# Adding half of the experts' results on GpSimd inside the attention, in a tuned one-core transformer kernel

## The chip, the cores and the metric

One core of a Trainium2 chip. The metric is the device time of one execution, from its first to its last instruction, in microseconds (us). TensorE is called PE below, VectorE DVE, ScalarE ACT, GpSimd POOL and the DMA queue's engine SP, as in the profile.

## The reference

The input x holds 8 batches of 512 rows of 128 channels. Two blocks follow each other, cut here to their steps:

```python
x = x + 0.5 * L0_ffn(layernorm(x))            # 8 experts, top 2, capacity 256
x = x + L0_attn(layernorm(x))                 # 16 heads, keys and values from a strided convolution
x = x + 0.5 * L0_ffn(layernorm(x))
x = x + 0.5 * L1_ffn(x)                       # its own causal attention, then 16 experts, top 2
x = x + L1_attn(x)                            # 16 heads, causal
x = x + 0.5 * L1_ffn(x)
```

A layer with experts gives every row the outputs of two experts, each times a gate: `out = out + combine[:, e][:, None] * ye`. The second block works on twice as many shorter sequences in the reference's own setup, but all calls here get (8, 512, 128).

## The kernel before

All of x stays in SBUF, as 32 tiles of 128 rows (four a batch). The program runs blocks one after the other; each ends with a barrier for all engines: experts, attention 1 (with convolution), experts, attention 2 (causal, the one inside the first L1_ffn, whose rows are normalised twice: once for the residual, once for the projections), experts, attention 3 (two attentions in a row, causal, 16 batches counted together), experts, and an end block that adds the last results and stores them.

**Experts.** `moe` ends with SP loading each row's two expert outputs back from DRAM, into the tiles xn and hid (`k.back`), 512 rows a batch. `k.rv[:, 4]` and `k.rv[:, 5]` hold the gates. Their addition into x is left to the block that follows.

**Attention.** `attention` is written as one program per engine. The unit of work is (batch b, group g of four heads), u = 4b + g, with 4 units a batch. For each unit PE computes the scores twice: first as row maxima (`max_tile`, L373 with the masks of L358), which DVE reduces (L657), and later as score products (`score_chunk`, L482) transposed, whose exponentials ACT writes (L530), and which PE multiplies with the values (L427). The maxima of a unit go PE transpose (L382), ACT copy (L562), a split into three bf16 parts on POOL (`max_split`, L767 to L773), and by SP into three rows of the query operand in SBUF (`put_max`, L872); the unit's first score product waits for them. A query and a key are themselves split into three bf16 parts (`split` on POOL, `split_first_keys` on DVE for batch 0), written to DRAM (`write_parts`, L854) and loaded back, laid out by group, by `load(b, g)` (L864), which also gates the maxima of that unit.

`order(u)` lists what happens in unit u: score chunk i, then the maxima tile i of unit u + 2 in another bank of PSUM, then the events whose number in the table `when` is i. PE, ACT and DVE all walk through the same list and each does its share. Chunks number 8 in attention 1 and 12 in the causal ones. Three PSUM banks take the maxima in turn, so that PE's tile i needs DVE's tile i - 3. POOL and SP have hand-written loops: POOL's unit u is `max_split(u + 1)`, then copies of value rows (`spread`), then one of: normalising batch b + 2 (g = 0), adding the output bias to its residual rows (`add_bias`, g = 1), splitting its queries and keys (g = 3). SP starts with

```python
            load(0, 0)
            load(0, 1)
            put_max(0)
            load(0, 2)
            load(0, 3)
            write_parts(1, 0)
```

**The entry.** Before the units DVE brings the batches in, in the groups 0, 1, 2 to 3 and 4 to 7 (`ENTRY_GROUPS`). `enter` adds the two gated results of each batch (`combine`, L251, four tiles each), takes means and variances (`moments`, L145 and L148) and ends with a chain of small operations for 1/sqrt (`deviations`, L156 and L115 to L119; twice over in attention 2, L160 to L164). `norm(b)` writes the normalised rows to transpose (xa) and, in attention 2, the residual rows (hid). Batches from 2 on are normalised on POOL. DVE's order is: enter 0, norm 0, enter 1, (convolve 0), norm 1, split_first_keys, value rows of batch 0, (convolve 1), enter the group 2 to 3, the maxima of unit 0, enter the group 4 to 7, the maxima of unit 1, then the units. The rows of batch 4 are first needed by POOL in unit 8.

## Time and profile before

| | |
|---|---|
| median of 3 runs | 2228.93 us (2227.15 to 2235.24) |
| the profiled execution | 2219.2 us |
| its span | 2217.5 us |
| PE busy | 1635.7 us (74%) |
| DVE busy | 1380.3 us (62%) |
| POOL busy | 1014.6 us (46%) |
| ACT busy | 979.6 us (44%) |

The span runs from the first to the last instruction of the profiled execution; the time beside it is what the device reports for the same execution. Attention 1 begins at about 150 us, attention 2 at 613 and attention 3 at 1254. A line of a timeline merges neighbouring instructions of one kind: its start, its length, engine, line, operation, what it writes and reads, the number of instructions, and in brackets the idle time of the engine before it with what ended it. In a list of waits stand the total, the number of times and the longest.

### The profile page before, as it was taken

To read this page: it belongs to the slowest core of one execution; us is meant where nothing else is said; L and a number is where in the kernel's file an instruction comes from. 1 tells how busy PE (TensorE), PEld (TensorE's weight loads), DVE (VectorE), ACT (ScalarE), POOL (GpSimd) and SP (SyncE) were. 2 spreads that over 40 slices of the span, in tenths; PEclk is the share of its full clock that TensorE was granted. 3 is DMA by queue.
4 is the path that set the end of the run, shared out by engine and by line. 5 is a ranking of instruction groups with operands and counts; after the bars stand their busy time and mean duration, and the time that the engine had idled before them with its cause. 6 is when DMAs were issued, how large, how long until landed. Compare 5 with 4: busy or idle time off the path is not lost. (4 is left out here: it accounts for less than half of the span.)

```text
span 2217.5 us, 45287 instructions
## 1 busy us (share of the span) xinstructions
PE 1635.7 (74%) x16814; PEld 929.4 (42%) x16816; DVE 1380.3 (62%) x3344; ACT 979.6 (44%) x2064; POOL 1014.6 (46%) x1706
## 2 busy tenths in 40 slices
PE   4434778873637999982687359999999999836872
PEld 3321333332514656651333135555656556523331
DVE  8538667746188777757321497777777777474213
ACT  1112566651214766661222127667666767511220
POOL 1233365530523657430577334536556674305772
PEclk9975899985858999996898669999999999867996
DMA  6242222210432323300244322332323233002444
GB/s 199 65 126 74 57 70 72 76 38 27 139 86 60 103 79 84 103 22 24 62 102 87 104 84 75 92 85 75 103 71 92 79 89 98 22 24 58 95 86 129
DMA packets 226872, 178.20 MB, mean 80 GB/s; under 512 B 33447, under 2 KB 215599, under 8 KB 226272
## 3 DMA queue, kind: packets, MB, share of 16 engines
q1 hardware_dynamic: 211232, 154.74, 24.6%
q0 software_dynamic: 10240, 17.96, 4.0%
q8 instruction: 135, 2.21, 0.4%
q10 hardware_dynamic: 5184, 2.63, 0.4%
q14 instruction: 81, 0.66, 0.1%
HBM read 104.34 MB, written 72.35 MB: 80 GB/s over the span
## 5 line engine op out<-in xcount | busy, mean ns | idle before, releaser
L657 DVE TENSOR_REDUCE mx<-PS 128x2 f32<-128x512 f32 (+3 forms) x1408 | 787.6, 611 | 255.5 <-PE PS L358 171.3
L530 ACT ACTIVATE pt<-PS 128x512 f32<-128x512 f32 (+2 forms) x1408 | 667.1, 533 | 363.7 <-PE PS L358 263.4
L373 PE MATMUL PS<-ka,qa 48*128 48x256 bf16 (+3 forms) x2048 | 503.6, 308 | 86.7 <-DVE mx L657 80.1
L482 PE MATMUL PS<-qa,ka 51*128 51x512 bf16 (+3 forms) x1792 | 485.2, 319 | 31.3 <-DMA qa<-nm 31.2
L358 PE MATMUL PS<-mask_q,identh 64*128 64x128 bf16 (+1 forms) x3072 | 354.9, 206 | 0.0
L427 PE MATMUL PS<-pt,vs 128*32 128x512 f32 (+3 forms) x3584 | 348.6, 482 | 0.0
L358 PE MATMUL PS<-mask_k,identh 64*128 64x64 bf16 (+1 forms) x3072 | 343.3, 202 | 0.0
L1174 POOL DMA_INDIRECT pt<-xn_rows,idx x160 | 165.3, 1033 | 333.7 <-DVE idx L1109 286.1
L767 POOL CAST nm<-nm 16x128 bf16<-16x128 f32 x128 | 36.0, 281 | 593.3 <-ACT nm L562 581.2
L358 PEld LDWEIGHTS PS<-mask_k,identh 64*128 64x128 bf16 x3072 | 270.3, 95 | 54.1 <-issue 1.8
L358 PEld LDWEIGHTS PS<-mask_q,identh 64*128 64x128 bf16 x3072 | 275.3, 97 | 26.5 <-issue 6.8
L482 PEld LDWEIGHTS PS<-qa,ka 51*128 51x128 bf16 x1792 | 166.7, 94 | 262.9 <-issue 153.6
L1025 ACT ACTIVATE pt<-PS,f1b 128x512 f32<-128x512 f32 x128 | 88.0, 687 | 314.3 <-PE PS L981 314.3
L373 PEld LDWEIGHTS PS<-ka,qa 48*128 48x128 bf16 x2048 | 173.8, 95 | 107.1 <-DVE mx L657 90.8
L991 PE MATMUL PS<-pt 128*128 128x512 f32 (+1 forms) x384 | 158.4, 558 | 0.0
L981 PE MATMUL PS<-pt 128*128 128x512 f32 (+1 forms) x384 | 153.0, 544 | 3.1 <-DVE pt L1137 2.0
L427 PEld LDWEIGHTS PS<-pt,vs 128*32 128x32 f32 x3584 | 81.4, 109 | 90.2 <-issue 39.4
L981 PEld LDWEIGHTS PS<-pt 128*128 128x128 f32 x384 | 76.4, 200 | 71.4 <-issue 62.7
L1145 DVE COPY qa<-PS 128x512 f32<-128x512 f32 (+1 forms) x48 | 28.9, 603 | 115.6 <-PE PS L991 115.6
L991 PEld LDWEIGHTS PS<-pt 128*128 128x128 f32 x384 | 74.3, 204 | 56.7 <-issue 54.1
L1183 POOL DMA_INDIRECT y_rows<-pt,idx x80 | 79.7, 996 | 38.4 <-issue 22.0
L391 PE MATMUL PS<-ident,xa 128*128 128x128 f32 x128 | 24.1, 320 | 97.0 <-DVE xa L188 80.2
(212 smaller groups left out, 2363.0 us busy)
## 6 DMA issues: line engine op xcount, KB each, us to landing
pt<-in_f_w SPq DMA_DIRECT2D x96, 256.0 KB, 3.2
q_parts<-parts SPq DMA_DIRECT2D x192, 128.0 KB, 2.4
qa<-q_parts SPq DMA_DIRECT2D x256, 96.0 KB, 2.4
k_parts<-parts SPq DMA_DIRECT2D x144, 128.0 KB, 2.4
ka<-k_parts SPq DMA_DIRECT2D x192, 96.0 KB, 2.4
xn_rows<-xn SPq DMA_DIRECT2D x32, 256.0 KB, 2.3
xn<-y_rows SPq DMA_DIRECT2D x32, 256.0 KB, 4.8
hid<-y_rows SPq DMA_DIRECT2D x32, 256.0 KB, 5.4
```

The lines of the kernel that those rows point to most:

```text
L358: mm = pe.matmul(PS[:, bank, col + lo:col + hi], k.identh[half * HALF:(half + 1) * HALF, j, :], table[half * HALF:(half + 1) * HALF, j, lo ...
L373: mm = pe.matmul(PS[:, bank, i * n:(i + 1) * n], k.qa[rows, b % 2, g, h // 2, qb * P:(qb + 1) * P], k.ka[rows, b % 2, g, h // 2, 0:n], sta ...
L427: mm = pe.matmul(PS[32 * h:32 * h + 32, O_BANK, q0:S], k.vs[:, g, kb, h, :], k.pt[:, u % 2, at[c] + i * n:at[c] + (i + 1) * n], start=(kb ...
L482: mm = pe.matmul(PS[:, bank, i * n:(i + 1) * n], k.ka[rows, b % 2, g, h // 2, kb * P:(kb + 1) * P], k.qa[rows, b % 2, g, h // 2, q0:S], st ...
L530: nc.scalar.activation(k.pt[:, u % 2, at[c]:at[c] + len(heads) * n], PS[:, SC_BANK + c % RING, 0:len(heads) * n], ACT.Exp, scale=SCORE_SCA ...
L657: nc.vector.tensor_reduce(out, PS[:, MX_BANK + t % RING, 0:len(heads) * n] .rearrange("p (h n) -> p h n", n=n), AX.X, ALU.max).then_inc(s. ...
L767: pool.tensor_copy(hi, full).then_inc(s.nm_hi.h, 1)
L981: pe.matmul(PS[:, H_BANK + f, 0:capacity], k.w1[:, par, f * P:(f + 1) * P], k.xeT[:, par, 0:capacity], start=True, stop=True).then_inc(s.h ...
L991: mm = pe.matmul(PS[:, YT_BANK, 0:capacity], k.w2[:, par, f, :], k.hT[:, par, f, 0:capacity], start=(f == 0), stop=(f == FC - 1))
L1025: nc.scalar.activation(k.hT[:, e % 2, f, 0:capacity], PS[:, H_BANK + f, 0:capacity], GELU, bias=w.b1[:, e * FC + f:e * FC + f + 1]).then_i ...
L1174: pool.indirect_dma_start(k.xe[e % RING_E][:, t, :], None, k.xn_dram[:, :], bass.IndirectOffsetOnAxis(k.idx[:, 0, n:n + 1], 0), bounds_che ...
L1183: pool.indirect_dma_start(k.y_rows[:, :], bass.IndirectOffsetOnAxis(k.idx[:, 1, n:n + 1], 0), k.ys[e % RING_E][:, t, :], None, bounds_chec ...
```

## The change

The results of batches 4 to 7 are no longer added by DVE in the entry. POOL adds them in units 1, 2, 5 and 6 (`LATE_ENTRY`), one batch each, in `add_results`: for each of the two results, the rows times their gates, then x plus these rows, as four operations on 128x512. DVE takes the batch's statistics a unit later ("late2", behind chunk 6 of a causal unit and chunk 4 of the other kind), and the 1/sqrt chain for all four in unit 8 ("late_root", behind chunk 0). The bias additions of batches 0 and 1 (`add_bias`) move on POOL from the end of unit 0 to a place ahead of batch 1's query split, and wait, in attention 2, for a semaphore of their own. In `norm` on DVE the rows to transpose are written ahead of the residual rows.

```diff
+    LATE_ENTRY = {1: 4, 2: 5, 5: 6, 6: 7}
...
+                "late0": 0, "late2": 6, "late_root": 0}
...
+                "late0": 0, "late2": 4, "late_root": 0}
...
+        if u in LATE_ENTRY:
+            events += [("late0", LATE_ENTRY[u])]
+        if u - 1 in LATE_ENTRY:
+            events += [("late2", LATE_ENTRY[u - 1])]
+        if u == max(LATE_ENTRY) + 2:
+            events += [("late_root", 3)]
...
+            def entry(step, b):
+                if step < 2:
+                    combine(nc, k, dve, seg(b).src, b, step)
+                else:
+                    if b in LATE_ENTRY.values():
+                        dve.wait_ge(*s.late_combined.at(b - min(LATE_ENTRY.values()) + 1))
+                    else:
+                        dve.wait_ge(*s.combined.at(2 * b + 2))
+                    chain.link(moments(nc, k, chain, seg(b).src, b))
+
+            def entry_deviations(group):
+                first, n = ENTRY_GROUPS[group]
+                deviations(nc, k, chain, columns(first, n), seg(0).twice).then_inc(s.st_ready.h, 1)
...
-                if twice:
-                    normalise(nc.vector, k, src, b, k.rstd, lambda t: here(dst, b)[:, t * P:(t + 1) * P])
                 normalise(nc.vector, k, src, b, k.rstd2 if twice else k.rstd,
                           lambda t: k.xa[:, t, :]).then_inc(s.xa_ready.h, 1)
+                if twice:
+                    normalise(nc.vector, k, src, b, k.rstd,
+                              lambda t: here(dst, b)[:, t * P:(t + 1) * P]).then_inc(s.base_ready.h, 1)
...
             enter(2)
-            for t in range(NMX):
-                max_tile(0, t)
-            enter(3)
-            for t in range(NMX):
-                max_tile(1, t)
+            for u in range(2):
+                for t in range(NMX):
+                    max_tile(u, t)
...
+                    elif name == "late2":
+                        entry(2, n)
+                    elif name == "late_root":
+                        entry_deviations(n)
...
-                pool.wait_ge(*s.xa_ready.at(b + 1))
+                pool.wait_ge(*(s.base_ready if seg(b).twice and b < 2 else s.xa_ready).at(b + 1))
...
+            def add_results(b):
+                four = lambda tile: here(tile, b).rearrange("p (t c) -> p t c", c=C)
+                pool.wait_ge(*s.gathered[b].at(16 * 2))
+                for c in range(2):
+                    rows, gates = four(k.back[c]), k.rv[:, 4 + c, columns(b)].unsqueeze(2).to_broadcast([P, TB, C])
+                    steps.link(pool.tensor_tensor(rows, rows, gates, ALU.mult))
+                    last = pool.tensor_tensor(four(seg(b).src), four(seg(b).src), rows, ALU.add)
+                    if c == 0:
+                        steps.link(last)
+                last.then_inc(s.late_combined.h, 1)
...
             for g in range(G):
                 spread(0, g)
+            add_bias(0)
+            add_bias(1)
             split(0, 1)
...
+                if u in LATE_ENTRY:
+                    add_results(LATE_ENTRY[u])
...
-                if u == 0:
-                    add_bias(0)
-                    add_bias(1)
```

What stands on DVE at the start of attention 3, before: the reductions of unit 0, and then the first two of four batches brought in (L657 is the reduction).

```order
L657 TENSOR_REDUCE mx<-PS 128x1 x8
L657 TENSOR_REDUCE mx<-PS 128x2 x4
L251 SCALAR_TENSOR_TENSOR x<-xn,rv,x 128x128 x4
L251 SCALAR_TENSOR_TENSOR x<-hid,rv,x 128x128 x4
L145 BN_STATS st<-x 128x6 x4
L148 BN_AGGR mv<-st 128x2 x4
L251 SCALAR_TENSOR_TENSOR x<-xn,rv,x 128x128 x4
L251 SCALAR_TENSOR_TENSOR x<-hid,rv,x 128x128 x4
L145 BN_STATS st<-x 128x6 x4
L148 BN_AGGR mv<-st 128x2 x4
```

The same place in the changed kernel, where the reduction is L679: units 0 and 1, and then what was reduced for unit 2.

```order
L679 TENSOR_REDUCE mx<-PS 128x1 x8
L679 TENSOR_REDUCE mx<-PS 128x2 x4
L679 TENSOR_REDUCE mx<-PS 128x1 x8
L679 TENSOR_REDUCE mx<-PS 128x2 x4
L679 TENSOR_REDUCE mx<-PS 128x1 x8
L679 TENSOR_REDUCE mx<-PS 128x2 x4
L669 COPY vst<-PS 128x512
L679 TENSOR_REDUCE mx<-PS 128x1 x6
L687 RECIPROCAL rec<-PS 128x16
L691 TENSOR_TENSOR ctx<-PS,rec 128x4x32
```

Nothing stands between the reductions of units 0, 1 and 2 any more; the statistics (L145, L148) come back one batch at a time in units 2, 3, 6 and 7.

POOL in attention 3 before, in units 0 (its last two rows here) and 1: after normalising batch 2, two bias additions; then unit 1 with one.

```order
L188 TENSOR_SCALAR xa<-x,mv,rstd 128x128 x4
L800 TENSOR_TENSOR x<-x,a1ob 128x512 x2
L767 CAST nm<-nm 16x128
L769 TENSOR_TENSOR nm<-nm 16x128
L771 CAST nm<-nm 16x128
L773 TENSOR_TENSOR nm<-nm 16x128
L756 COPY vs<-vst 128x16x8
L800 TENSOR_TENSOR x<-x,a1ob 128x512
L767 CAST nm<-nm 16x128
```

POOL at the same place in the changed kernel (the split of maxima is L791 to L797, the value copy L780, the bias addition L824).

```order
L188 TENSOR_SCALAR xa<-x,mv,rstd 128x128 x4
L791 CAST nm<-nm 16x128
L793 TENSOR_TENSOR nm<-nm 16x128
L795 CAST nm<-nm 16x128
L797 TENSOR_TENSOR nm<-nm 16x128
L780 COPY vs<-vst 128x16x8
L831 TENSOR_TENSOR xn<-xn,rv 128x512
L832 TENSOR_TENSOR x<-x,xn 128x512
L831 TENSOR_TENSOR hid<-hid,rv 128x512
L832 TENSOR_TENSOR x<-x,hid 128x512
L824 TENSOR_TENSOR x<-x,a1ob 128x512
L791 CAST nm<-nm 16x128
```

The two bias additions are gone from unit 0, and four additions of results stand in unit 1 ahead of the next split of maxima.

## Rows read from the trace of the kernel before

**Rows 1.** Waits on PE: tile, line <- releaser: total us, times, longest
```profile
PE PS L373 <- DVE mx L657: 80.1, 27, 19.7
```

**Rows 2.** Timeline of DVE, block of batches 4 to 7: start, length, line, operation
```profile
185.90 1.13 DVE L251 SCALAR_TENSOR_TENSOR x<-xn,rv,x 128x128 f32<-128x128 f32 x4
...
203.05 4.87 DVE L657 TENSOR_REDUCE mx<-PS 128x2 f32<-128x512 f32 x8
...
656.06 1.13 DVE L251 SCALAR_TENSOR_TENSOR x<-xn,rv,x 128x128 f32<-128x128 f32 x4
...
676.79 6.38 DVE L657 TENSOR_REDUCE mx<-PS 128x1 f32<-128x512 f32 x12
...
1290.15 1.13 DVE L251 SCALAR_TENSOR_TENSOR x<-xn,rv,x 128x128 f32<-128x128 f32 x4
...
1308.58 6.37 DVE L657 TENSOR_REDUCE mx<-PS 128x1 f32<-128x512 f32 x12
```

**Rows 3.** Timeline of PE: first row-maximum products of unit 2, each attention
```profile
207.46 0.58 PE L373 MATMUL PS<-ka,qa 48*128 48x256 bf16 x2 [0.25 <-DVE mx L657]
...
682.65 0.58 PE L373 MATMUL PS<-ka,qa 48*128 48x512 bf16 x1
...
1314.44 0.58 PE L373 MATMUL PS<-ka,qa 48*128 48x512 bf16 x1
```

**Rows 4.** Timeline of SP's DMA issues around the start of each attention
```profile
191.29 1.27 SPq L864 DMA_DIRECT2D ka<-k_parts  x2
...
661.38 0.90 SPq L864 DMA_DIRECT2D ka<-k_parts  x2
...
1278.67 0.78 SPq L864 DMA_DIRECT2D ka<-k_parts  x2
...
1292.81 1.70 SPq L872 DMA_DIRECT2D qa<-nm  x3
...
1295.47 0.90 SPq L864 DMA_DIRECT2D ka<-k_parts  x2
```

**Rows 5.** Timeline of PE, third attention, first product of unit 0
```profile
1281.42 0.61 PE L373 MATMUL PS<-ka,qa 48*128 48x512 bf16 x2 [2.26 <-DMA ka<-k_parts]
```

**Rows 6.** Timelines of DVE and POOL, third attention, the same microseconds
```profile
1277.12 3.88 DVE L251 SCALAR_TENSOR_TENSOR x<-hid,rv,x 128x128 f32<-128x128 f32 x4
...
1277.80 1.15 POOL L743 TENSOR_TENSOR rest<-q,parts 128x512 f32<-128x512 f32 x1
...
1279.70 1.15 POOL L748 TENSOR_TENSOR parts<-rest,parts 128x512 bf16<-128x512 f32 x1
```

**Rows 7.** Timeline of POOL: idle ahead of a split of maxima; price rows
```profile
276.36 0.28 POOL L767 CAST nm<-nm 16x128 bf16<-16x128 f32 x1 [10.11 <-ACT nm L562]
...
763.69 3.11 POOL L188 TENSOR_SCALAR hid<-x,mv,rstd 128x128 f32<-128x128 f32 x4
...
734.29 1.27 POOL L800 TENSOR_TENSOR hid<-hid,afob 128x512 f32<-128x512 f32 x1
...
1334.87 0.28 POOL L767 CAST nm<-nm 16x128 bf16<-16x128 f32 x1 [5.08 <-ACT nm L562]
```

**Rows 8.** Timeline of DVE, second attention: value copies, maxima, statistics
```profile
691.48 0.69 DVE L647 COPY vst<-PS 128x512 f32<-128x512 f32 x1 [0.53 <-PE PS L409]
...
718.51 1.35 DVE L657 TENSOR_REDUCE mx<-PS 128x2 f32<-128x512 f32 x3 [1.36 <-PE PS L358]
...
729.03 0.69 DVE L647 COPY vst<-PS 128x512 f32<-128x512 f32 x1 [0.53 <-PE PS L409]
...
742.44 0.86 DVE L145 BATCH_NORM_STATS2 st<-hid 128x6 f32<-128x128 f32 x4
...
767.73 0.69 DVE L647 COPY vst<-PS 128x512 f32<-128x512 f32 x1 [0.53 <-PE PS L409]
```

**Rows 9.** Timeline of DVE: last root chain begins; a tap of a convolution
```profile
672.93 0.17 DVE L156 TENSOR_SCALAR dev<-mv 128x16 f32<-128x16 f32 x1
...
232.07 0.48 DVE L637 SCALAR_TENSOR_TENSOR cv<-xnT,a0cw,cv 128x256 f32<-128x256 f32 x1
```

More of the change, by code:

```diff
@@ L286, in attention @@
         when = {"value_p": 2, "max_T": 2, "o_out": 2, "nm": 2, "o_T": 5, "value0": 8, "x_T": 8, "k": 8, "ctx_T": 8,
-                "q": 11, "v": 11, "out": 11, "value1": 11, "moments": 4, "f_moments": 4, "f_T": 8, "f_l": 11}
+                "q": 11, "v": 11, "out": 11, "value1": 11, "moments": 4, "f_moments": 4, "f_T": 8, "f_l": 11,
+                "late0": 0, "late2": 6, "late_root": 0}
         early, late = ((0,), (1,)), (2, 3)
@@ L292, in attention @@
         when = {"value_p": 2, "max_T": 2, "o_out": 2, "nm": 2, "o_T": 4, "x_T": 5, "k": 5, "ctx_T": 5, "value0": 6,
-                "q": 7, "v": 7, "out": 7, "moments": 3, "f_moments": 3, "f_T": 5, "f_l": 7}
+                "q": 7, "v": 7, "out": 7, "moments": 3, "f_moments": 3, "f_T": 5, "f_l": 7,
+                "late0": 0, "late2": 4, "late_root": 0}
         early, late = ((0,),), (1,)
@@ L601, in enter @@
                 for b in range(first, first + n):
-                    for c in range(2):
-                        combine(nc, k, dve, seg(b).src, b, c)
-                    dve.wait_ge(*s.combined.at(2 * b + 2))
-                    chain.link(moments(nc, k, chain, seg(b).src, b))
-                deviations(nc, k, chain, columns(first, n), seg(0).twice).then_inc(s.st_ready.h, 1)
+                    for step in range(3):
+                        entry(step, b)
+                entry_deviations(group)
             def later_moments(b):
@@ L899, in attention @@
     counts = {
-        s.ln_step: k.entry_steps, s.pl_step: k.pool_steps, s.st_ready: len(ENTRY_GROUPS), s.mo_ready: NB - B, s.fm_ready: B - 1, s.combined: 2 * B, s.xn_stored: 16 * B,
+        s.ln_step: k.entry_steps, s.pl_step: k.pool_steps, s.st_ready: len(ENTRY_GROUPS), s.mo_ready: NB - B, s.fm_ready: B - 1,
+        s.base_ready: 2 * seg(0).twice, s.combined: 2 * (B - len(LATE_ENTRY)), s.late_combined: len(LATE_ENTRY), s.xn_stored: 16 * B,
         s.xa_ready: NB, s.ob_added: NB, s.xT_full: NB, s.xT_free: NB, s.q_full: NB,
@@ L1240, in __init__ @@
         self.ln_step = new("ln_step")
-        self.pl_step = new("pl_step")
+        self.late_combined = new("late_combined")
+        self.pl_step, self.base_ready = new("pl_step"), new("base_ready")
         self.st_ready, self.mo_ready, self.fm_ready = new("st_ready"), new("mo_ready"), new("fm_ready")
```

## The prediction, made before the changed kernel ran

> **What bounds the kernel now.** I read the page first: a span of 2217.5 us, PE busy for 74% of it, DVE for 62%. Neither is full on average, so some stretches must be bound by something else. Then the waits on PE: row-maximum products (L373) waited 80.1 us for DVE's reductions, 27 times, the longest 19.7 us [rows 1]. Then DVE's timeline at the start of each attention: between the reductions of unit 0 and those of unit 1 stands the block in which DVE adds the results of batches 4 to 7 and takes their statistics, from 185.90 to 203.05, 656.06 to 676.79 and 1290.15 to 1308.58 [rows 2]. That is 17.15 + 20.73 + 18.43 = 56.3 us, in which PE, ACT, POOL and the DMA queue run dry: unit 1's maxima are behind it. Everything else in an attention is a regular pattern of units (9 to 10 us each), where PE is the limit and DVE is close behind it.
>
> **What the change removes.** The block goes from its place; the question is what is late next. Unit 1's reductions now follow those of unit 0 at once, and unit 0's score products follow them on PE. But each score chunk is followed by a maximum product of unit 2, and unit 2's rows are loaded by SP only behind the three transfers of unit 0's maxima. So the next releaser is that load. In the third attention those transfers are issued at 1292.81 and unit 2's key rows at 1295.47 to 1296.37 [rows 4]. From the end of such an issue to the first product that needs it passed 1281.42 - (1278.67 + 0.78) = 1.97 us [rows 4, 5]. Unit 2's first maximum product could thus start at 191.29 + 1.27 + 1.97 = 194.5, at 661.38 + 0.90 + 1.97 = 664.3 and at 1295.47 + 0.90 + 1.97 = 1298.3, and it started at 207.46, 682.65 and 1314.44 [rows 3, 4]: **12.9 + 18.4 + 16.1 = 47.4 us** to be had, not 56.3. Behind it, the order on SP (write of batch 1's query parts, then unit 1's maxima) has the same length as the unit 0 work around it, so the shift is kept.
>
> **The bias additions moved up.** They now run on POOL right behind the first copies of value rows, while DVE adds the results of batches 2 and 3 (in the first attention, while it convolves batch 1). DVE's additions can't run beside POOL's work: four of them (L251) take 1.13 us alone [rows 2], and 3.88 us at 1277.12, when POOL was splitting queries [rows 6]. That is 2.75 us lost to three POOL operations, some 0.9 us each, as if each addition waited for the POOL operation in progress to end. Replaying DVE's order against two more POOL operations of 1.27 us [rows 7], and against the split that the delayed additions then run into, I get 2.8, 2.9 and 1.7 us for the three attentions, 7.4 us together. DVE's statistics of batch 2 and 3 set when unit 0's reductions begin, so this is on the path. Bounds: nothing, if the operations miss each other; 2 x 1.27 us for the two additions and as much again for the split, 5.1 us an attention. I take 7.4, since the additions begin within a microsecond of each other. That leaves 47.4 - 7.4 = **40.0 us**. The Trainium skill has the mechanism (SBUF — State Buffer, "Who interferes with whom"): a GpSimd instruction and a VectorE instruction with two operands in SBUF exclude each other for a whole instruction. By that rule the trace agrees, and reductions that read PSUM are left alone, as they are here.
>
> **The additions on POOL.** Four operations of 128x512 for each of batches 4 to 7. POOL's addition of a broadcast bias to 128x512 takes 1.27 us [rows 7], so 4 x 1.27 + 0.2 of links = 5.3 us a batch. They stand behind the split of maxima in units 1, 2, 5 and 6. In the twelve such places of the three attentions POOL sat idle before the next split for 5.08 us (the shortest, at 1334.87) to 10.11 us (the longest, at 276.36) [rows 7], 88.7 us in all. So they are hidden, with 0.2 us missing in one place, and cost nothing. Lower bound of one operation: 1.15, the split's subtraction [rows 6]; upper bound: 3.11, the normalising of the same 512 columns in four pieces [rows 7]. I take 1.27, which has the same shape and also a broadcast operand. If this cover were gone, the next split of maxima would be late, then its transfers, then the unit's first score product. The Trainium skill speaks against the move (GPSIMD Engine Reference, "Engine selection": elementwise work with two inputs belongs on VectorE, GpSimd being about half as fast). The rows agree on the speed, 5.3 us against the 2.3 us of DVE's additions; by the rule alone the change would lose 3 us a batch, which holds only where POOL is waited for; that is the last of the rivals.
>
> **The statistics, a unit later, on DVE.** 1.24 us a batch (0.86 and 0.38) in units 2, 3, 6 and 7. What such an insertion costs is seen inside the second attention: from one value copy to the next are 37.55 us without (691.48 to 729.03) and 38.70 us with one batch's statistics (729.03 to 767.73) [rows 8], so 1.15 us of 1.24 come through. That one stands behind the fifth reduction, where products come without a break. The new ones stand behind the seventh, ahead of the place where PE does value products and DVE idles for up to 1.36 us (718.51) [rows 8]. I take 0.1 us each for three of four, and the full 1.15 where a unit has statistics already (unit 6 of the second attention, unit 7 of the third): 1.45 each. In the first attention, with spare time on DVE, 0.2 each, 0.8. Together **3.7 us**, bounds 0 and 12 x 1.24 = 14.9.
>
> **The root chain** of batches 4 to 7, now behind the first reduction of unit 8. It took 676.79 - 672.93 = 3.86 us in the second attention [rows 2, 9], 19 operations of 0.2 us; the single root of the other two has 8, 1.6 us. PE may run about 0.6 us ahead there, so I take 3.3, 1.0 and 0.8: **5.1 us**, bounds 0 and 7.1.
>
> **Convolutions.** In the first attention those of batches 2 and 3 fall into the units in which POOL now adds. Their taps take 0.48 us [rows 9], have operands in SBUF alone, and each of three can wait for a POOL operation: up to 3.8 us of DVE twice. Reductions have slack behind them, so I take 1.0 us of PE each: **2.0 us**, bounds 0 and 7.6.
>
> **The rows to transpose ahead of residual rows** bring batch 0's transposes forward by 1.1 us in the second attention only. I cost it at nothing: the path there runs through DVE, which does the same work in either order before it splits batch 0's keys.
>
> **Sum.** 40.0 - 3.7 - 5.1 - 2.0 = **29.2 us**. Against the profiled execution, 2219.2 us, that makes 2190.0. That execution lies 9.7 us under the median of the runs, 2228.93, so I forecast 2228.9 - 29.2 = **2199.7 us** for the median.
>
> **Rivals.**
> - Full cover: POOL's moved additions miss DVE's, and the statistics and roots fit into idle time. For it: DVE idles in every unit. Against it: rows 6 and rows 8. The gain is 47.4 us, 2181.5.
> - DVE as the limit: inside the units every microsecond given to DVE comes through, 14.9 + 7.1, and the convolutions wait half of their bound, 3.8. For it: 1.15 of 1.24 us came through in rows 8. Against it: the idle time at 718.51. The gain is 40.0 - 25.8 = 14.2, 2214.7.
> - The block hid another wait: if unit 1's own rows had not landed, its maxima would wait in its place. Half of 29 would be left, 2214 or more, up to no change. Against it: SP issues them right behind unit 0's, which left at 1278.67 [rows 4], over 10 us before unit 1's turn.
> - Slower: POOL becomes the limit. Were an operation with the gates to cost 3.11 us, a batch would take 12.6 us, the twelve together 151.7, 63.0 over the idle 88.7, each microsecond of it ahead of a split of maxima. 29.2 - 63.0 is a loss of 33.8 us, 2262.7. It decides from 48 x t + 2.4 = 88.7 + 29.2 on, so from t = 2.4 us an operation. Against it: three kinds of POOL operation of this shape take 1.15 to 1.27.
>
> **How the numbers follow.** The forecast's case has 0.70, full cover 0.11, DVE as the limit 0.11, the hidden wait 0.04, POOL as the limit 0.04. A measurement of this kernel can tell 0.5%, 11.1 us, from no change. Faster by more: 0.70 + 0.11 + 0.09 of the 0.11 of DVE as the limit, whose gain lies barely over it, = 0.90; the rest of that case and the hidden wait, 0.06, lie within it; slower 0.04. The range reaches from full cover, 2182, to DVE as the limit, 2215.
>
> **What would show it.** In the changed profile DVE's two runs of reductions for units 0 and 1 should touch; PE's first score product of unit 0 should come 12 to 18 us earlier against the first reduction, followed by a wait of 2 to 3 us for rows of unit 2; L251 should be 16 instructions fewer an attention on each of two tiles, and POOL should show 48 new operations near 1.27 us with idle left behind them. Units 2, 3, 6, 7 should last no more than 0.2 us longer, but for one in each causal attention. The forecast is wrong if the POOL operations take over 2 us, if unit 0's first reduction is not delayed, or if the value-to-value time of batches 0 and 1 grows by over 3 us.

## The result, and the profile after

The changed kernel took 2205.03 us (median of 4 executions, 2201.14 to 2208.02) against 2229.26 us of the kernel before on the same chip: a ratio of 0.9876, with a 95% interval from 0.9844 to 0.9907, so 24.2 us less by the medians. Two later jobs, on two chips, timed the same kernel again: 2243.02 against 2277.26 us (0.9881 [0.9827, 0.9936], 34.2 us less) and 2199.27 against 2230.39 us (0.9840 [0.9801, 0.9879], 31.1 us less). The mean of the three differences is 29.8 us; forecast were 29.2. The ratios are those on record and not the quotients of these medians, which would be 0.9891, 0.9850 and 0.9860: differences of a few microseconds between two kernels can't be read from either.

The profiled execution of the changed kernel is the slowest of its four (2208.02 us, span 2206.0 us), that of the kernel before the fastest of its own (2219.2 us). Their spans differ by only 11.5 us, and the stages have to be read one by one.

The waits on PE, which answer to [rows 1]: tile and line, what ended the wait, total us, times, longest.

```profile
PE PS L382 <- DVE mx L679: 44.6, 31, 7.1
PE PS L491 <- DMA qa<-nm: 25.2, 19, 3.4
```

L382 is the row-maximum product that was L373, L679 the reduction that was L657. The total went from 80.1 to 44.6 us, the longest from 19.7 to 7.1. The second row was 31.2 us in the kernel before.

The entry of attention 2 on DVE, as a timeline (start, length, line, operation, and in brackets the idle time before it):

```profile
614.93 1.14 DVE L251 SCALAR_TENSOR_TENSOR x<-xn,rv,x 128x128 f32<-128x128 f32 x4 [17.88 <-PEq L973]
...
640.46 3.16 DVE L251 SCALAR_TENSOR_TENSOR x<-hid,rv,x 128x128 f32<-128x128 f32 x4
...
644.98 3.48 DVE L251 SCALAR_TENSOR_TENSOR x<-xn,rv,x 128x128 f32<-128x128 f32 x4
...
654.70 6.38 DVE L679 TENSOR_REDUCE mx<-PS 128x1 f32<-128x512 f32 x12
662.25 6.39 DVE L679 TENSOR_REDUCE mx<-PS 128x1 f32<-128x512 f32 x12 [1.17 <-PE PS L367]
670.69 1.93 DVE L679 TENSOR_REDUCE mx<-PS 128x1 f32<-128x512 f32 x3 [2.05 <-PE PS L367]
...
678.74 0.69 DVE L669 COPY vst<-PS 128x512 f32<-128x512 f32 x1 [0.53 <-PE PS L418]
```

The reductions of units 0 and 1 (12 each) are 1.17 us apart, where the block of additions and roots lay before [rows 2]. Before unit 2's DVE waits 2.05 us, the remainder that the forecast left for the landing of unit 2's rows. Two groups of additions take 3.16 and 3.48 us instead of 1.14: the first runs against POOL's two bias additions (640.55 to 643.21), the second against the query split behind them (subtractions at 644.99 and 646.89), as the forecast had it. The value copy of batch 1 starts 678.74 - 614.93 = 63.8 us after the attention's first addition. In the kernel before it was 78.7, up to the copy at 691.48 [rows 8].

What became of the additions, as groups of POOL and of DVE (count | busy us, mean ns of one | idle before):

```profile
L831 POOL TENSOR_TENSOR xn<-xn,rv 128x512 f32<-128x512 f32 x12 | 12.4, 1031 | 0.0
L832 POOL TENSOR_TENSOR x<-x,xn 128x512 f32<-128x512 f32 x12 | 15.3, 1272 | 0.9
...
L251 DVE SCALAR_TENSOR_TENSOR x<-hid,rv,x 128x128 f32<-128x128 f32 x80 | 29.0, 425 | 0.7
```

There are 48 new operations on POOL (these two groups and two more for the second result, 12.5 and 15.3 us), 1.16 us each, against 1.27 forecast. DVE has 48 instructions of L251 fewer on each tile. One batch on POOL:

```profile
721.26 1.03 POOL L831 TENSOR_TENSOR xn<-xn,rv 128x512 f32<-128x512 f32 x1
722.36 1.26 POOL L832 TENSOR_TENSOR x<-x,xn 128x512 f32<-128x512 f32 x1
723.71 1.04 POOL L831 TENSOR_TENSOR hid<-hid,rv 128x512 f32<-128x512 f32 x1
724.83 1.28 POOL L832 TENSOR_TENSOR x<-x,hid 128x512 f32<-128x512 f32 x1
726.06 1.27 POOL L824 TENSOR_TENSOR hid<-hid,afob 128x512 f32<-128x512 f32 x1
728.50 0.28 POOL L791 CAST nm<-nm 16x128 bf16<-16x128 f32 x1 [1.17 <-ACT nm L571]
```

A batch takes 726.06 - 721.26 = 4.8 us, and a bias addition follows. The next split of maxima (L791) still finds POOL idle for 1.17 us: it waits for ACT, not for POOL. The same holds in all twelve places of this trace, with 0.26 to 4.53 us of idle time left; the least in the third trace is 0.10.

**The stages.** The table gives us, worked out from the timelines of DVE, for attentions 1 / 2 / 3: from the attention's first addition to the value copy of batch 1, from there to batch 2's (units 1 to 4), to batch 3's (units 5 to 8), and from the last value copy to the last output addition. "Again" and "third" are the two later traces of the same changed kernel.

| stage | before | after | after, again | after, third |
|---|---|---|---|---|
| entry to value 1 | 65.3 / 78.7 / 69.1 | 53.4 / 63.8 / 55.6 | 53.2 / 64.4 / 54.8 | 53.2 / 65.1 / 54.7 |
| units 1 to 4 | 33.8 / 37.6 / 36.6 | 38.4 / 37.3 / 36.8 | 36.1 / 37.5 / 37.1 | 36.3 / 36.6 / 37.2 |
| units 5 to 8 | 39.4 / 38.7 / 38.8 | 40.6 / 46.5 / 44.1 | 42.3 / 46.8 / 41.1 | 45.0 / 47.9 / 41.1 |
| from there to the last value copy | 148.4 / 159.7 / 469.8 | 146.9 / 160.2 / 469.8 | 144.7 / 159.7 / 469.8 | 143.0 / 159.8 / 469.4 |
| end | 73.5 / 79.0 / 83.1 | 82.9 / 82.4 / 80.5 | 80.2 / 78.9 / 79.0 | 82.4 / 79.3 / 81.6 |

The entry gives 40.3, 40.7 and 40.1 us in the three traces. Units 1 to 8 take back 18.7, 16.0 and 19.2 of it, most of that in units 5 to 8 (14.3, 13.3 and 17.1). But what attention 1 loses there (1.2, 2.9 and 5.6 us) it wins back behind them: its next stage is 1.5, 3.7 and 5.4 us shorter than before, while that of the other two stays. Up to their last value copies the three attentions together are 22.6, 28.4 and 26.8 us shorter than before. Why attention 1 gives the time back was not looked into.

**Where units 5 to 8 lose it.** The chain of roots in unit 8 of attention 2, on DVE, with the POOL and PE rows of the same microseconds:

```profile
746.35 0.69 DVE L679 TENSOR_REDUCE mx<-PS 128x1 f32<-128x512 f32 x1 [0.68 <-PE PS L367]
746.96 0.16 DVE L156 TENSOR_SCALAR dev<-mv 128x16 f32<-128x16 f32 x1
747.16 0.52 DVE L115 TENSOR_SCALAR rstd<-dev 128x16 int32<-128x16 int32 x1
...
747.92 1.02 DVE L118 SCALAR_TENSOR_TENSOR tmp<-tmp,dev 128x16 f32<-128x16 f32 x1
...
752.55 2.81 DVE L679 TENSOR_REDUCE mx<-PS 128x1 f32<-128x512 f32 x5
```

```profile
747.73 1.18 POOL L772 TENSOR_TENSOR parts<-rest,parts 128x512 bf16<-128x512 f32 x1
...
753.29 0.50 PE L382 MATMUL PS<-ka,qa 48*128 48x384 bf16 x1 [4.75 <-DVE mx L679]
```

The chain takes 752.55 - 746.96 = 5.59 us; in the block it took 3.86 [rows 2, 9]. One operation at 747.92 lasts 1.02 us instead of 0.17 and ends with POOL's subtraction at 748.9. PE then waits 4.75 us for a reduction, and its next products take 0.50 us instead of 0.32. The windows say why (us, busy time of each engine, granted clock as a fraction of full speed):

```profile
750.00:754.00 4.00, 0.71 (x5) 0.54 (x7) 3.62 (x15) 0.00 (x0) 2.11 (x5) 0.77 0.18 47
754.00:758.00 4.00, 4.00 (x36) 2.88 (x34) 3.25 (x8) 2.03 (x4) 4.00 (x6) 0.50 0.74 200
758.00:762.00 4.00, 4.00 (x54) 2.62 (x53) 1.76 (x4) 1.96 (x5) 0.99 (x2) 0.88 0.65 183
```

During the wait the clock is halved, to 1.2 GHz, and stays so while PE is at work again up to about 759. So the chain is paid for twice: as a wait and as slow products behind it.

### The profile page after: what moved, and what is told of

It reads as the page before. It is cut to its first block and busy times, and to the rows that moved or that the text cites. A ratio compares the mean times of both kernels' runs of the same rounds, so it can differ in the third digit from the quotient of the medians.

```text
span 2206.0 us, 45242 instructions
## 1 busy us (share of the span) xinstructions
PE 1664.4 (75%) x16814; PEld 939.9 (43%) x16816; DVE 1361.0 (62%) x3248; ACT 981.7 (45%) x2064; POOL 1072.8 (49%) x1754
## 5 line engine op out<-in xcount | busy, mean ns | idle before, releaser
L679 DVE TENSOR_REDUCE mx<-PS 128x2 f32<-128x512 f32 (+3 forms) x1408 | 788.4, 612 | 257.3 <-PE PS L367 171.7
L382 PE MATMUL PS<-ka,qa 48*128 48x256 bf16 (+3 forms) x2048 | 508.4, 310 | 54.8 <-DVE mx L679 44.6
L491 PE MATMUL PS<-qa,ka 51*128 51x512 bf16 (+3 forms) x1792 | 491.7, 323 | 26.2 <-DMA qa<-nm 25.2
L436 PE MATMUL PS<-pt,vs 128*32 128x512 f32 (+3 forms) x3584 | 355.3, 490 | 0.0
L791 POOL CAST nm<-nm 16x128 bf16<-16x128 f32 x128 | 36.1, 282 | 518.2 <-ACT nm L571 504.7
L491 PEld LDWEIGHTS PS<-qa,ka 51*128 51x128 bf16 x1792 | 167.3, 94 | 264.6 <-issue 159.8
L382 PEld LDWEIGHTS PS<-ka,qa 48*128 48x128 bf16 x2048 | 174.0, 95 | 77.3 <-DVE mx L679 53.1
L1220 POOL DMA_INDIRECT y_rows<-pt,idx x80 | 79.8, 997 | 38.8 <-issue 22.6
```

The costliest lines, as they stand in the source:

```text
L382: mm = pe.matmul(PS[:, bank, i * n:(i + 1) * n], k.qa[rows, b % 2, g, h // 2, qb * P:(qb + 1) * P], k.ka[rows, b % 2, g, h // 2, 0:n], sta ...
L436: mm = pe.matmul(PS[32 * h:32 * h + 32, O_BANK, q0:S], k.vs[:, g, kb, h, :], k.pt[:, u % 2, at[c] + i * n:at[c] + (i + 1) * n], start=(kb ...
L491: mm = pe.matmul(PS[:, bank, i * n:(i + 1) * n], k.ka[rows, b % 2, g, h // 2, kb * P:(kb + 1) * P], k.qa[rows, b % 2, g, h // 2, q0:S], st ...
L679: nc.vector.tensor_reduce(out, PS[:, MX_BANK + t % RING, 0:len(heads) * n] .rearrange("p (h n) -> p h n", n=n), AX.X, ALU.max).then_inc(s. ...
L791: pool.tensor_copy(hi, full).then_inc(s.nm_hi.h, 1)
L1220: pool.indirect_dma_start(k.y_rows[:, :], bass.IndirectOffsetOnAxis(k.idx[:, 1, n:n + 1], 0), k.ys[e % RING_E][:, t, :], None, bounds_chec ...
```

## The experiments

The theory at this point: the entry went as forecast; what came back is mainly the chain, through its length, through POOL, and through PE's clock. The rivals: the late statistics, POOL's additions, or the convolutions. Kernels of one job ran on one chip with the kernel before, and only their times are compared with one another. The first job holds the next four, and not the changed kernel itself, which is known there only by its ratio in another job, 0.9876. The ratios of the first three (0.9850 to 0.9855) can't be told from it, so these three are read by their stages, which are also set against the first trace of the changed kernel.

**Bias additions put back** behind unit 0.

```diff
@@ POOL, entry
                 spread(0, g)
-            add_bias(0)
-            add_bias(1)
             split(0, 1)
@@ POOL, units
+                if u == 0:
+                    add_bias(0)
+                    add_bias(1)
```

> The bias additions of batches 0 and 1 are put back at the end of POOL's unit 0; all else is as in the changed kernel. Theory (POOL's operations hold up DVE's additions in the entry): from an attention's first addition of results to the first reduction of unit 0 it takes 33.4, 39.8 and 31.2 us in the changed kernel and 31.5, 37.0 and 29.7 before; it goes back to the latter, and the whole is some 6 us faster than the changed kernel, about 2199 us. Rival (the entry is longer for another reason, such as the order of the normalising): the entry stays within 0.5 us of the changed kernel's and the time at 2205. Second rival (the additions cost the same in unit 0, ahead of the split of unit 2's maxima): the entry is shorter, but the first value copies of the units come no earlier.

Measured: 2197.88 against 2227.05 us, 0.9851 [0.9812, 0.9889]. The first reduction came after 31.5 / 37.1 / 29.7 us, as in the kernel before, instead of 33.4 / 39.8 / 31.2: 1.95 + 2.66 + 1.45 = 6.1 us. The value copy of batch 1 came 2.7, 1.3 and 2.1 us earlier, also 6.1. The additions in attention 3:

```profile
1271.79 1.14 DVE L251 SCALAR_TENSOR_TENSOR x<-xn,rv,x 128x128 f32<-128x128 f32 x4
1272.96 3.88 DVE L251 SCALAR_TENSOR_TENSOR x<-hid,rv,x 128x128 f32<-128x128 f32 x4
```

One of four is long again, as in [rows 6]; in the changed kernel there are two. The term of 7.4 us in the forecast (2.8, 2.9 and 1.7) was the right mechanism and measured 6.1.

**Roots in pieces.** The chain is cut into two groups of two batches, and its operations, 2 to 4 at a time, stand behind reductions of units 3 to 7 and 8 to 11.

```diff
-    ENTRY_GROUPS = ((0, 1), (1, 1), (2, 2), (4, 4))
+    ENTRY_GROUPS = ((0, 1), (1, 1), (2, 2), (4, 2), (6, 2))
...
+    ROOTS = {(3, 1): (3, 3), (4, 0): (3, 4), (4, 1): (3, 3), (5, 0): (3, 2), (5, 1): (3, 2), (6, 1): (3, 2), (7, 1): (3, 3),
+             (8, 0): (4, 4), (8, 1): (4, 2), (9, 0): (4, 2), (9, 1): (4, 2), (10, 1): (4, 2), (11, 0): (4, 4), (11, 1): (4, 3)}
```

> The root chain of batches 4 to 7 is cut in two (4 and 5, 6 and 7) and its operations, 19 or 8 a chain, are spread by twos to fours over units 3 to 7 and 8 to 11, behind the ninth and the last reduction of a unit. Theory (the chain in one piece in unit 8 starves PE for some 5 us, and the clock falls behind it): unit 8 of attentions 2 and 3 is 7.7 and 5.3 us shorter than in the changed kernel, other units stay within 0.5 us, and the whole is 11 to 15 us faster, 2190 to 2194 us. Rival (unit 8 is long because POOL waits for the root before it normalises batch 4): the same gain in unit 8, but POOL's next splits come late when the pieces end late; not told apart by the time, but by PE's waits, which would name DMA of the maxima. Second rival (DVE's work counts wherever it stands): the gain is under 4 us.

Measured: 2196.57 against 2227.05 us, 0.9850 [0.9813, 0.9886]. Units 5 to 8 took 36.6 / 40.7 / 38.8 us, so 4.0, 5.8 and 5.3 less than in the changed kernel's first trace, and in attention 3 what they took before the change. The clock in the same microseconds of attention 2:

```profile
752.00:756.00 4.00, 4.00 (x57) 2.83 (x56) 3.70 (x10) 2.51 (x6) 4.00 (x6) 1.00 0.38 101
```

PE is busy without a break and the clock stays at 2.4 GHz, although this kernel executes more root operations than the other. Not the work but its standing in one piece was the cost, in attentions 2 and 3. The first rival falls with the wait shown above, which in the changed kernel was for DVE's reduction and not for the transfer of the maxima. In attention 1 the 4.0 us are no gain: from there to the last value copy it took 151.5 us, 4.6 more than in the changed kernel. The total fell short of the expected 2190 to 2194 us.

**Rows of unit 2 first.** SP issues the loads of units 2 and 3 ahead of the maxima of unit 0 [rows 4].

```diff
             load(0, 1)
-            put_max(0)
             load(0, 2)
             load(0, 3)
+            put_max(0)
```

> SP issues the rows of units 2 and 3 ahead of unit 0's maxima. Theory (once the block is gone, unit 2's rows are what comes last): DVE's idle time between unit 1's and unit 2's reductions, 2.5, 2.05 and 1.4 us in the changed kernel, falls to 0.3 to 1, and the whole is 3 to 5 us faster, about 2201 us. Rival (unit 0's maxima, in the same queue, would be as late): the idle time stays and the time is 2205.

Measured: 2196.22 against 2227.05 us, 0.9855 [0.9817, 0.9894]. DVE's idle time before the first reduction of unit 2 fell from 2.50, 2.05 and 1.41 us to under 0.3 in all three attentions, as the theory said. Value copy 1 came 3.2, 1.1 and 1.7 us earlier, 6.0 together. So the landing of unit 2's rows did end the entry's wait, as the forecast's 47.4 us assume, and this order takes a part of that bound away.

**All three mends.**

> All three together. Theory: 6 + 13 + 4 us less than the changed kernel, 2180 to 2184 us. Rival (they share one wait): no better than the best of the three.

Measured: 2189.33 against 2227.05 us, 0.9804 [0.9767, 0.9840]. Entry 49.2 / 60.2 / 52.0, units 5 to 8 37.8 / 40.7 / 38.8 us. PE's waits for DVE's reductions fell to 29.4 us, from 44.6. The expected 2180 to 2184 us were missed; it is still the lowest of the four, so the rival that they share one wait is not borne out.

The second job ran on a chip on which the kernel before takes 2277.26 us. The changed kernel as it is was its yardstick:

> The changed kernel once more, for a second profile of it. Theory: the time from an attention's first addition to the end of unit 0 (its value copy) is 53.4, 63.8 and 55.6 us again within 0.5, and units 5 to 8 of attention 2 take 46.5 us again; what differs from run to run, by up to 8 us in the whole, is TensorE's granted clock, in the tails of the attentions above all. Rival: the stretches themselves differ, and then no single profile says what the root chain costs.

Measured: 2243.02 us, 0.9881 [0.9827, 0.9936]. The entries came within 0.8 us of the first trace, units 5 to 8 of attention 2 took 46.8 us (46.5 in the first), but those of attentions 1 and 3 differ by 1.7 and 3.0. So the rival holds for these stages: one profile does not say what the chain costs in attention 3.

**POOL's work in the units doubled**: four more products of rows and gates behind each batch, on rows that nobody reads any more, 4.5 us.

```diff
                 last.then_inc(s.late_combined.h, 1)
+                pool.wait_ge(*s.late_combined.at(b - min(LATE_ENTRY.values()) + 1))
+                for _ in range(2):
+                    for c in range(2):
...
+                        steps.link(pool.tensor_tensor(rows, rows, gates, ALU.mult))
```

> POOL repeats the two products of rows and gates twice for each of batches 4 to 7, after the sums and into rows that nobody reads any more: 4 x 1.03 + 0.2 us more a batch, 4.3, so some 9.2 us for a batch in place of 4.9. Over the idle time of the twelve places (5.08 to 10.11 us) that is 23 us too much in all. Theory (a late split of maxima has some slack of its own before its unit begins): under half of it comes through, 0 to 10 us, 2205 to 2215. Rival (every microsecond over the idle time is paid, as the prediction's slower case had it): 23 us slower than the changed kernel, about 2228, and the waits of L491 for the maxima grow by as much.

Measured: 2265.92 us, 0.9956 [0.9927, 0.9985], so 22.9 us slower than the changed kernel beside it. That is the rival's result. Units 1 to 4 took 3.0, 4.4 and 6.1 us more, units 5 to 8 1.5, 2.6 and 4.6. In attention 2, POOL and then PE:

```profile
710.13 1.04 POOL L840 TENSOR_TENSOR hid<-hid,rv 128x512 f32<-128x512 f32 x1
711.23 0.28 POOL L791 CAST nm<-nm 16x128 bf16<-16x128 f32 x1
```

```profile
715.57 0.39 PE L491 MATMUL PS<-qa,ka 51*128 51x512 bf16 x1 [2.01 <-DMA qa<-nm]
```

The split follows on POOL's last product without idle time, its transfer is late, and PE waits 2.01 us. All waits of L491 for the maxima grew by 10.7 us only (38.6 against 27.9), so not the whole loss stands in them, as the rival had it. The additions of the change lie hidden, as forecast, but the room behind them is nearly used up: at 4.8 us a batch they hold up no split, and at 9.3 much is lost. The rival "POOL as the limit" had the right mechanism, and only the price of an operation, 1.16 us and not 3.11, kept it away.

**A ladder of chains.** In attention 3, behind the first reduction of units 20, 24, 28 and 32, stand 4, 8, 12 and 19 operations on 16 columns that nobody reads.

```diff
+    LADDER = {20: 4, 24: 8, 28: 12, 32: 19}
...
+                    elif name == "ladder":
+                        for _ in range(n):
+                            chain.link(nc.vector.tensor_tensor(k.tmp[:, 0:16], k.dev[:, 0:16], k.dev[:, 0:16], ALU.mult))
```

> In attention 3, chains of 4, 8, 12 and 19 small dependent operations on DVE (0.2 us each, on a scratch tile, 0.8, 1.6, 2.5 and 3.9 us) are added behind the first reduction of units 20, 24, 28 and 32, where the changed kernel has only its regular pattern. Theory (PE runs some 0.6 us ahead, then waits, and a wait of some length costs clock on top): these units last 0.2, 1.0 to 2, 2 to 4 and 6 to 8 us longer. Rival 1 (DVE's time comes through one to one and no more): 0.8, 1.6, 2.5 and 3.9. Rival 2 (unit 8 was long because of what POOL does there): under 1 us each.

Measured (one execution; it is read unit by unit): the four rungs on DVE, then PE's waits behind them, then the clock behind the second.

```profile
1522.48 1.41 DVE L747 TENSOR_TENSOR tmp<-dev 128x16 f32<-128x16 f32 x4
...
1562.43 2.49 DVE L747 TENSOR_TENSOR tmp<-dev 128x16 f32<-128x16 f32 x8
...
1604.97 3.65 DVE L747 TENSOR_TENSOR tmp<-dev 128x16 f32<-128x16 f32 x12
...
1651.01 5.42 DVE L747 TENSOR_TENSOR tmp<-dev 128x16 f32<-128x16 f32 x19
```

```profile
1524.68 0.33 PE L385 MATMUL PS<-ka,qa 48*128 48x384 bf16 x1 [0.61 <-DVE mx L682]
...
1565.70 0.33 PE L385 MATMUL PS<-ka,qa 48*128 48x384 bf16 x1 [1.68 <-DVE mx L682]
...
1609.57 0.50 PE L385 MATMUL PS<-ka,qa 48*128 48x384 bf16 x1 [3.02 <-DVE mx L682]
...
1657.21 0.50 PE L385 MATMUL PS<-ka,qa 48*128 48x384 bf16 x1 [4.61 <-DVE mx L682]
```

```profile
1566.00:1570.00 4.00, 4.00 (x41) 2.97 (x38) 3.74 (x9) 2.07 (x4) 4.00 (x6) 0.66 0.23 61
```

Against the same units of the changed kernel, from one reciprocal of row sums to the next, and with the unit behind it where that is longer too, the rungs cost 1.2, 3.8, 7.4 and 9.0 us, 21.4 together. The stretch from the fourth value copy to the last grew by 491.4 - 469.8 = 21.6, so nothing of it was won back.

| operations | DVE, us | PE's wait, us | mean clock of the slowest 4 us behind | cost, us |
|---|---|---|---|---|
| 4 | 1.41 | 0.61 | 1.00 | 1.2 |
| 8 | 2.49 | 1.68 | 0.66 | 3.8 |
| 12 | 3.65 | 3.02 | 0.50 | 7.4 |
| 19 | 5.42 | 4.61 | 0.50 | 9.0 |

PE's wait is the rung's length less 0.6 to 0.8 us, which is how far it was ahead. The shortest rung costs its own length less 0.2 us. The longer ones cost 1.3 to 3.7 us more than their length, and that is where the clock falls. All four cost more than the theory said (0.2, 1 to 2, 2 to 4 and 6 to 8): it took 0.2 us an operation, and they took 0.29 to 0.35. Both rivals fall, the second with every rung and the first with the three longer ones. The chain of attention 2 (5.59 us, cost 7.6 to 8.6 in three traces) is the last rung.

**Statistics earlier**: the late statistics behind the fifth reduction instead of the seventh.

```diff
-                "late0": 0, "late2": 6, "late_root": 0}
+                "late0": 0, "late2": 4, "late_root": 0}
```

> In the causal attentions the late statistics stand behind the fifth reduction of their unit (chunk 4), where the regular ones stand, in place of the seventh. Theory (the place decides: ahead of the value products DVE has slack): units 2, 3, 6 and 7, which the late statistics lengthened by 0.0 to 0.15 us, become 0.9 to 1.2 us longer each, more in unit 6 of attention 2 and unit 7 of attention 3, which have two. Rival (the statistics are cheap anywhere, and the 1.15 us read in the profile before had another cause): no unit changes by over 0.3 us.

Measured (one execution, read by units): a single batch's statistics cost 1.2 us in unit 2 of the causal attentions, where they cost 0.0 to 0.15 behind the seventh. In unit 6 of attention 2, where two batches' now stand together, unit 6 took 15.3 us instead of 9.8 (from reciprocal to reciprocal, which also holds the next batch's statistics):

```profile
735.23 0.86 DVE L145 BATCH_NORM_STATS2 st<-x 128x6 f32<-128x128 f32 x4
...
736.54 0.87 DVE L145 BATCH_NORM_STATS2 st<-hid 128x6 f32<-128x128 f32 x4
```

```profile
738.33 0.39 PE L382 MATMUL PS<-ka,qa 48*128 48x256 bf16 x1 [2.14 <-DVE mx L679]
```

A wait of 2.14 us, and products of 0.39 instead of 0.27 us behind it. Units 1 to 4 of the two causal attentions, with one batch's statistics in two of them, took 1.6 and 2.0 us more than in the changed kernel beside it. So the theory holds: the place behind the seventh reduction has room, that behind the fifth has none.

The third job:

**The additions on DVE in the units**: `add_results` leaves POOL, and DVE adds one result behind the seventh reduction and one behind the last.

```diff
-                "late0": 0, "late2": 6, "late_root": 0}
+                "late0": 6, "late1": 11, "late2": 6, "late_root": 0}
...
-                if u in LATE_ENTRY:
-                    add_results(LATE_ENTRY[u])
```

> VectorE adds the results of batches 4 to 7 itself: in units 1, 2, 5 and 6 of each attention two additions (1.15 us) behind the seventh max chunk and two behind the last; the statistics stay where the change has them, so in units 2 and 6 additions and statistics of two batches form one stretch of 2.4 us without a reduction. Theory (what counts is the longest stretch of VectorE's work without a reduction: up to about 1.3 us it costs 0 to 1 us, from about 2 us on PE's wait is over 1.5 us, its clock falls and it costs 4 to 6 us): in the causal attentions units 1 and 5 lose 0 to 1.5 us, units 2 and 6 lose 3 to 6 us each, the first attention half of that; 15 to 28 us slower than the changed kernel. Rival (every microsecond given to VectorE comes through once): 2.3 us in each of the twelve units, 27.6, evenly spread, with no unit above 3. Second rival (VectorE has room and GpSimd's additions hold nothing): within 5 us of the changed kernel.

Measured: 2206.53 against 2230.39 us, 0.9893 [0.9856, 0.9929]; the changed kernel beside it took 2199.27, so 7.3 us less. My theory missed: it named 15 to 28. Units 1, 2, 5 and 6 of the causal attentions lost about 1.0 us each, also those with 2.4 us of additions and statistics in a row:

```profile
730.98 1.13 DVE L251 SCALAR_TENSOR_TENSOR x<-xn,rv,x 128x128 f32<-128x128 f32 x4
732.03 0.87 DVE L145 BATCH_NORM_STATS2 st<-x 128x6 f32<-128x128 f32 x4
```

```profile
733.96 0.23 PE L382 MATMUL PS<-ka,qa 48*128 48x128 bf16 x1 [0.64 <-DVE mx L676]
```

PE waits 0.64 us and its clock stays up. That points to the length of a stretch less the room of its place, and not its length alone: behind the first or the fifth reduction 2.5 us make PE wait 1.7 to 2.1, behind the seventh 0.6. It also divides the change's gain: that the additions left the entry is worth most of it, that POOL does them rather than DVE about 7 us of some 30, which is less than the intervals of the two ratios can tell for certain. Up to the last value copies the three attentions took 10.8 us more than in the changed kernel beside it, and 2.6 of that is unit 8, with the slower clock, of attention 3, which differs between traces of one kernel (see the end of the next section).

**The changed kernel a third time, and the three mends a second time.**

> The changed kernel again, beside the next one on the same chip. 22 to 27 us faster than the kernel before; it serves to tell what the three mends together are worth against it.

> The three mends together again. In the traces their stages are shorter than those of the changed kernel by 11.4 us up to the value copy of batch 1 and by 13.9 us in units 5 to 8, 25 us together, while the medians of two chips gave only 13 us. If the rest is chance in how the clock is granted behind the attentions, this run is 20 to 25 us faster than the changed kernel beside it; if the gain is given back there as a rule, 10 to 14 us, and the time from the last value copy of an attention to its last output addition is longer than the changed kernel's in all three attentions.

Measured: 2199.27 us, 0.9840 [0.9801, 0.9879], and 2181.67 us, 0.9768 [0.9729, 0.9807]. So the mends gain 17.6 us over the changed kernel and 48.7 over the one before. The 31.1 us of the first are more than its expected 22 to 27, and 17.6 lies between the two expectations of the second. Up to value copy 1 the mends gain 3.9, 5.4 and 1.8 us, in units 5 to 8 7.9, 7.2 and 2.2; units 1 to 4 of attention 1 are 3.4 us longer, and the end is shorter in one attention and longer in two. No rule of giving back shows in the ends. It shows in attention 1: from value copy 3 to the last it took 150.7 us against 143.0, so the 7.9 us won in its units 5 to 8 were nearly all lost again, as with the roots in pieces. Of the expected 25 us, 15 are left up to the last value copies.

**The order of the rows undone.**

```diff
-                normalise(nc.vector, k, src, b, k.rstd2 if twice else k.rstd,
-                          lambda t: k.xa[:, t, :]).then_inc(s.xa_ready.h, 1)
                 if twice:
...
+                normalise(nc.vector, k, src, b, k.rstd2 if twice else k.rstd,
+                          lambda t: k.xa[:, t, :]).then_inc(s.xa_ready.h, 1)
```

> The changed kernel with residual rows written ahead of the rows to transpose again. Only the second attention writes both. Theory: its first transposes of batch 0 come 1.1 us later and nothing else, since VectorE does the same work before it splits batch 0's keys: within 2 us of the changed kernel. Rival: the second attention's entry gets longer by up to 1.1 us a batch, 2 to 4 us until its value copy of batch 1.

Measured: 2194.82 us, 0.9823 [0.9777, 0.9869], beside 0.9840 of the changed kernel: no difference that this can tell. In attention 2 the first reduction came after 39.62 us (39.75 with the change) and value copy 1 after 63.7 (63.8 to 65.1). This part of the change is worth nothing, as costed.

## Why the prediction was right, point by point

- **The entry, 40.0 us**: right. It gave 40.1 to 40.7 in three traces. Of its parts, the collisions were put at 7.4 and measured 6.1. By them and the rest, the full cover is 46.4 us where the forecast has 47.4. Moving the loads shows that unit 2's rows were the next bound. PE's first score product of unit 0 came 15.2, 19.5 and 17.2 us earlier behind the first reduction than before (12 to 18 were named).
- **The additions on POOL**: right in size (4.8 us a batch for 5.3) and in being hidden. The doubled work shows that the room was real but small. The Trainium skill (GPSIMD Engine Reference, "Engine selection") would leave such work on VectorE; here, by the run with the additions on DVE, the median is then 7.3 us higher, not lower: on POOL nobody waits for them.
- **Statistics, 3.7 us**: over-sized. Behind the seventh reduction they cost 0.0 to 0.15 us in every causal unit that can be read. The step that failed is "the full 1.15 where a unit has statistics already": two sets behind two different reductions do not add up. Where one set stands behind the fifth, the 1.15 of [rows 8] was right (1.2).
- **Root chain, 5.1 us**: mis-sized, the largest error. In attention 2 it cost 7.6 to 8.6 for 3.3, in attention 3 2.2 or 5.3 for 0.8, and in attention 1 nothing that lasted, for 1.0: together 9.9 to 12.9 us. The sum priced the chain by its length in the block less 0.6 us, for which it showed no row; the ladder bears that size out. Two things were missing: in unit 8 POOL splits keys, and the chain's operations wait for it (3.86 became 5.59 us, and 1.56 became 2.41 in attention 3); and PE's wait costs it its clock. The upper bound of 7.1 us for the chain did not hold either, since it was the length of the work.
- **Convolutions, 2.0 us**: not settled. Units 1 to 4 of attention 1 lost 4.6, 2.3 and 2.5 us in three traces of one kernel, and all of attention 1 up to its last value copy 4.2, 1.4 and 2.5; no run took the convolutions away from POOL's additions. Read as units 1 to 4, the prediction's sign of being wrong ("grows by over 3 us") came up here in one trace of three.
- **The rivals**: the full cover would have needed a gain of 47.4 us; the mends reach 37.7 and 48.7 in two jobs, but with two orders of their own. DVE as the limit, 14.2 us, falls by the time and with the statistics; behind a unit's first reduction, though, the ladder shows that with chains of 8 operations and more even more than every microsecond comes through. The hidden wait falls with the rows of the entry: DVE waited 1.01, 1.17 and 1.17 us ahead of unit 1's reductions, not 10.
- **The sum**: 29.2 us against 24.2, 34.2 and 31.1 measured. By the stages up to the last value copies it is 22.6, 28.4 and 26.8. The forecast therefore owes some of its fit to chance: it put the statistics some 3 us too high and the chain 5 to 8 too low, and the two make up for each other in part. What is then left between the stages and the medians lies in the ends, which differ between executions (next point), and there is only one trace of the kernel before.

**What the executions differ by.** The end of attention 1 has the same work in both kernels. Before, then after (the same columns as above):

```profile
436.50:510.00 73.50, 53.06 (x375) 24.24 (x374) 33.83 (x76) 39.62 (x80) 23.21 (x64) 0.90 0.13 38
```

```profile
429.30:512.10 82.80, 63.70 (x374) 28.31 (x374) 33.69 (x76) 39.94 (x80) 23.34 (x64) 0.74 0.12 34
```

The mean clock was 0.90 in the one and 0.74 in the other, and this end took 73.5 and 82.9 us. That it is an effect of the change is not shown, and it is not excluded: the thirteen traces of the changed kernel and its variants had 75.3 to 82.9 us there (POOL doubled 75.8 at 0.81, the second run of the mends 75.3 at 0.85), and of the kernel before there is one trace. One wait shows such a difference within one kernel. In unit 8 of attention 3, after and after-third:

```profile
1379.21 0.33 PE L382 MATMUL PS<-ka,qa 48*128 48x384 bf16 x1 [1.56 <-DVE mx L679]
```

```profile
1374.32 0.33 PE L382 MATMUL PS<-ka,qa 48*128 48x384 bf16 x1 [1.56 <-DVE mx L679]
```

The wait is 1.56 us in both. Behind it the clock fell to 0.53 in the first and stayed at 1.00 in the second:

```profile
1380.00:1384.00 4.00, 4.00 (x35) 2.97 (x33) 3.50 (x8) 1.99 (x4) 2.72 (x4) 0.53 0.29 76
```

```profile
1375.00:1379.00 4.00, 4.00 (x53) 2.44 (x53) 3.37 (x8) 2.54 (x5) 2.80 (x4) 1.00 0.28 73
```

The unit took 12.7 and 9.7 us, 3 us for nothing that the program, the same in both, does differently. Eight traces in all have this wait (1.55 or 1.56 us), and behind it the clock fell in four. What decides between the two was not found.

## What to carry to other kernels

Work that is taken out of a block on the critical path should be put back in pieces, each behind an operation with room after it; the price of a piece is its length less that room, and a chain of small dependent operations in one piece is the dearest form. Price a wait of TensorE with the slow products behind it, and a small VectorE operation with what GpSimd does at that moment. Compare two traces by stages, follow a stage that got longer or shorter up to a common end before it is called a loss or a gain (attention 1 paid both back), and take several traces of one kernel before a difference of 3 to 9 us in a stage that the change does not touch is read as its effect.

## What the runs showed of the hardware

- TensorE's clock fell to 1.2 GHz during or behind each of the waits of 1.68, 2.01, 2.14, 3.02, 4.61 and 4.75 us shown above, in four of eight traces behind 1.55 or 1.56, and not behind 0.61 and 0.64. The length of the wait alone does not decide it: with POOL's work doubled PE waited 1.68 us up to 1358.48, and the clock was 1.00 in the 4 us before 1359 and in the 4 behind. On the ladder a fallen clock went with 1.3 to 3.7 us beyond the chain's own length.
- An operation of VectorE on only 16 columns, with operands in SBUF, waits for a GpSimd operation as large ones do: 1.02 us instead of 0.17 at 747.92. The Trainium skill has the rule (SBUF — State Buffer, "Who interferes with whom"), and by that rule the trace agrees: the shorter the operation, the larger the factor.
- GpSimd's product of 128x512 with a broadcast gate took 1.03 us, its addition of two such tiles 1.27, together half as fast as VectorE's fused form of both (2.3 us a batch against 4.8).
